# A two-block transformer kernel: first products by two tiles with the high parts first, router weights side by side, output-weight splits two steps later

## The reference

```
xn = layernorm(x)
x  = x + series_and_ffn(xn) + lora_top2(xn)          # block 0
xn = layernorm(x)
x  = x + attention(xn) + base_and_lora_routed(xn)    # block 1
```

## Time and profile before

| | us |
|---|---|
| median of 3 runs | 628.64 |
| lowest, highest | 627.43, 631.06 |
| the profiled execution | 631.41 |
| its span (first to last instruction) | 629.7 |
| mean granted clock of TensorE in it | 0.984 of full |

### The profile page before, as it was taken

How to read it: one execution, slowest core, us unless ns; L and a number is a source line. 1 busy time by engine, 2 the same in 40 slices (tenths; PEclk the granted TensorE clock), 3 DMA queues, 4 the chain that set the end, 5 groups by cost and what they waited for, 6 DMA issues and landing times.

```text
span 629.7 us, 9383 instructions
## 1 busy us (share of the span) xinstructions
PE 602.0 (96%) x3704; PEld 397.4 (63%) x3704; DVE 373.6 (59%) x553; ACT 293.3 (47%) x511; POOL 76.2 (12%) x106
## 2 busy tenths in 40 slices
PE   2999999999999999999999998999999999999996
PEld 2788888877888887687676764344444444534444
DVE  5667645237644324875845356568898888861225
ACT  3465524124523222423212114677787787756772
POOL 3000000000000000402211112121212122111210
PEclk9999999999999999999999998899999999969999
DMA  7424232312021212377914735161615440101003
GB/s 214 135 90 134 68 120 81 101 33 68 34 67 34 67 34 67 104 168 212 171 52 134 141 130 92 22 109 32 120 45 98 79 69 19 31 9 30 15 14 133
DMA packets 24067, 53.12 MB, mean 84 GB/s; under 512 B 8384, under 2 KB 8896, under 8 KB 24016
## 3 DMA queue, kind: packets, MB, share of 16 engines
q1 hardware_dynamic: 23736, 51.96, 32.3%
q0 software_dynamic: 288, 0.58, 0.4%
HBM read 39.63 MB, written 10.60 MB: 80 GB/s over the span
## 4 chain that ended last, share of the span: by engine, by line
PE 87%; ACT 5%; DVE 5%; issue 1%; DMA 1%; SPq 0%; DVEq 0%; ACTq 0%
PE bank L1289 12%; PE slot L1011 11%; PE slot L1013 10%; PE slot L1012 10%; PE bank L1272 10%; PE bank L1011 9%; PE bank L1013 8%; PE bank L1012 8%; PE slot L1183 6%; ACT probs L994 4%; PE slot L1191 2%; DMA x_sb<-in_x 1%; PE slot L1027 1%; PE slot L1272 1%; DVE maxcol L1637 1%
## 5 line engine op out<-in xcount | busy, mean ns | idle before, releaser
L994 ACT ACTIVATE probs<-bank 128x512 f32<-128x512 f32 (+2 forms) x294 | 144.2, 566 | 53.3 <-PE bank L1272 50.1
L1637 DVE TENSOR_REDUCE maxcol<-slot 128x2 f32<-128x1024 f32 (+2 forms) x112 | 125.1, 1142 | 31.2 <-PE slot L1183 16.2
L1011 PE MATMUL slot<-xt_hi,ring_hi 128*128 128x512 f32 (+2 forms) x248 | 98.3, 396 | 3.6 <-DVE xt_lo L1412 2.4
L1012 PE MATMUL slot<-xt_lo,ring_hi 128*128 128x512 f32 (+2 forms) x248 | 97.5, 393 | 0.0
L1013 PE MATMUL slot<-xt_hi,ring_lo 128*128 128x512 f32 (+2 forms) x248 | 97.4, 393 | 0.0
L1289 PE MATMUL bank<-probs,v_sb 128*32 128x512 f32 (+3 forms) x768 | 86.6, 525 | 0.1
L1272 PE MATMUL bank<-qst,kst 50*128 50x512 f32 (+3 forms) x275 | 74.5, 431 | 5.6 <-ACT probs L994 4.1
L1272 PEld LDWEIGHTS bank<-qst,kst 50*128 50x128 f32 x275 | 33.7, 193 | 63.7 <-ACT probs L994 51.5
L786 POOL TENSOR_SCALAR_AFFINE_SELECT probs<-probs 128x512 f32<-128x512 f32 x64 | 41.7, 652 | 188.0 <-ACT probs L994 187.9
L1637 DVE TENSOR_REDUCE maxrest<-slot 128x2 f32<-128x768 f32 (+3 forms) x48 | 49.8, 1045 | 21.9 <-PE slot L1191 21.7
L1183 PE MATMUL slot<-kst,qst 48*128 48x512 f32 (+3 forms) x288 | 57.0, 388 | 2.3 <-DVE negm L1650 2.0
(11 more groups left out here) (212 smaller groups left out, 851.2 us busy)
## 6 DMA issues: line engine op xcount, KB each, us to landing
stage<-in_stream SPq DMA_DIRECT2D x43, 512.0 KB, 3.5
qst<-heads_dram SPq DMA_DIRECT2D x12, 256.0 KB, 4.9
kst<-heads_dram SPq DMA_DIRECT2D x12, 256.0 KB, 7.9
heads_dram<-attn_hi SPq DMA_DIRECT2D x4, 512.0 KB
heads_dram<-attn_lo SPq DMA_DIRECT2D x4, 512.0 KB
out_y<-x_sb SPq DMA_DIRECT2D x8, 256.0 KB, 2.1
stage<-u_sb SPq DMA_DIRECT2D x56, 32.0 KB, 2.0
stage<-den_dram SPq DMA_DIRECT2D x14, 128.0 KB
```

The lines of the kernel that those rows point to most:

```text
L994: act.activation(probs[:, to:to + heads, 0:n], score_ps(b)[:, 0:heads * n].rearrange("p (h n) -> p h n", n=n), ACT.Exp, scale=HD ** -0.5). ...
L1011: pe.matmul(out_ap, a[0], b[0], start=start, stop=False)
L1012: pe.matmul(out_ap, a[0], b[1], start=False, stop=False)
L1637: dve.tensor_reduce(per_head[:, :, slots[0]:slots[-1] + 1], scores, AX.X, ALU.max).then_inc(S["max_free"], 1)
```

## The change

Four places. (1) Start: pairs 0 and 1 are turned into the four single banks instead of the slots; pair 0's copy on ACT and low part on DVE come ahead of pair 1's normalization; PE runs 20 transposes of the identity before turn(0) and 18 behind it; the first gate_up product is done for the 256 tokens of pair 0 first, high by high, then high weights by low tokens, then turn(1), then low weights by high tokens, then all of it for pair 1; weight item 2 is issued ahead of x tiles 4-7. (2) Half 1, chunk 0: two of the four take_outs move behind h_lo. (3) Router weights of block 1: high and low columns lie side by side (32 stationary columns), so high weights and low weights meet the high tokens in one matmul; the two parts are transposed and then added by a reduction; the eviction of the logits moves ahead of the value-weight splits. (4) Attention: wo0 is split at step 3 and wo1 at step 4 of group 0.

```diff
-SPLIT_AT = {(0, 1): "wo0", (0, 3): "wo1"}
+BEFORE_TURN, BEHIND_TURN = 20, 18
+SPLIT_AT = {(0, 3): "wo0", (0, 4): "wo1"}
 def psum_users():
-    users = [("x", 0), ("x", 1)]
+    users = []
...
-        lgt1 = probs[0:ROUTES_PAD, 0:2, :].rearrange("p a n -> p (a n)")
+        lgt1 = probs[0:2 * ROUTES_PAD, 0:2, :].rearrange("p a n -> p (a n)")
...
-            return slot_of(("x", q))[:, n, :] if q < 6 else bank[2 * (q - 6) + n][:, :]
+            return slot_of(("x", q))[:, n, :] if 2 <= q < 6 else bank[2 * (q % 2) + n][:, :]
...
             weights(1)
+            weights(2)
             sp.dma_start(x_sb[:, 4:8, :], x_in[4:8].rearrange("t p d -> p t d")).then_inc(S["x_landed3"], 16)
-            for n in range(2, item_at[("wv1", 0)] + 1):
+            for n in range(3, item_at[("wv1", 0)] + 1):
                 weights(n)
...
             std(0)
+            turned_hi(0)
             std(1)
-            turned_hi(0)
             split_hi(0)
             turned_hi(1)
+            split_hi(1)
             act.wait_ge(S["ratio_diff"], 1)
             act.activation(ratio[:], disc[:], ACT.Exp).then_inc(S["ratio_ready"], 1)
-            for n in range(1, 3):
-                split_hi(n)
+            split_hi(2)
...
+            def keep_clock(n):
+                for _ in range(n):
+                    pe.transpose(slot[1][:, 0, 0:P], ident[:], ident[:])
+
+            def first_gate_up():
+                n, hi, lo = ring_of("gate_up")
+                hi, lo = (t.rearrange("p (k m) -> p k m", k=KD) for t in (hi, lo))
+                ps = slot_of(("s", 0))
+                early = slice(0, 2 * P)
+
+                def part(w, x, start, stop):
+                    for out in range(2):
+                        for k in range(KD):
+                            pe.matmul(ps[:, out, early], w[:, k, out * P:(out + 1) * P], x[:, k, early],
+                                      start=start and k == 0, stop=stop and k == KD - 1)
+
+                pe.wait_ge(S["xt_hi_ready"], 1)
+                pe.wait_ge(S["w_hi"], 1)
+                part(hi, xt_hi, True, False)
+                pe.wait_ge(S["x_free"], 1)
+                part(hi, xt_lo, False, False)
+                turn(1)
+                pe.wait_ge(S["w_lo"], 1)
+                part(lo, xt_hi, False, True)
+                pe.wait_ge(S["x_free"], 2)
+                for out in range(2):
+                    last = from_xt(ps[:, out, 2 * P:HALF], (hi, lo), out * P, (out + 1) * P, 2 * P, 2 * P)
+                last.then_inc(S["s_ready"], 1)
+
             pe.wait_ge(S["ident_ready"], 2)
+            keep_clock(BEFORE_TURN)
             turn(0)
-            turn(1)
+            keep_clock(BEHIND_TURN)
...
             def route_logits(n):
-                return from_xt(slot_of(("r", 0))[0:ROUTES_PAD, n, :], (rw_hi, rw_lo), 0, ROUTES_PAD, n * HALF, HALF)
+                at = slice(n * HALF, (n + 1) * HALF)
+                for k in range(KD):
+                    pe.matmul(slot_of(("r", 0))[0:2 * ROUTES_PAD, n, :], rw[:, k].rearrange("p a n -> p (a n)"),
+                              xt_hi[:, k, at], start=(k == 0), stop=False)
+                    last = pe.matmul(slot_of(("r", 0))[0:ROUTES_PAD, n, :], rw[:, k, 0, :], xt_lo[:, k, at],
+                                     start=False, stop=(k == KD - 1))
+                return last
...
+                    src = logit[:, :, 0:routes]
+                    parts = wide(bank[0][:, 0:1], (2 * ROUTES_PAD, NT), (1, routes), (ROUTES_PAD, 2))
+                    then(dve.tensor_reduce(src, parts, AX.X, ALU.add))
...
             statistics(1)
+            turned_lo(0)
             invert_std(1)
             normalize(1)
-            turned_lo(0)
             split_lo(0)
             turned_lo(1)
+            split_lo(1)
             dve.wait_ge(S["vec_landed"], 64)
...
-            split_lo(1)
             split_lo(2)
...
                 if half == 1:
-                    for t in range(HT):
+                    for t in range(2):
                         take_out(t)
...
+                    if (half, c) == (1, 0):
+                        for t in range(2, HT):
+                            take_out(t)
                     if c == 0:
                         dve.wait_ge(S["l_a_ready"], half + 1)
                         route(HT, NE, half)
...
             for n in range(2):
                 first_lo(0, n)
+            dve.wait_ge(S["r_ready"], 1)
+            dve.tensor_scalar(lgt1, slot_of(("r", 0))[0:2 * ROUTES_PAD].rearrange("p a n -> p (a n)"),
+                              vec_sb[0:2 * ROUTES_PAD, VEC_ROUTER1:VEC_ROUTER1 + 1], None, ALU.add
+                              ).then_inc(S["r_free"], 1)
             for n in range(2):
                 split_lo(item_at[(f"wv{n}", 0)])
```

More of the change, by code:

```diff
@@ L816, in turned_hi @@
                 act.wait_ge(S["x_turned"], q + 1)
-                if q < 6:
+                if 2 <= q < 6:
                     act.activation(xt_hi[:, :, t:t + 2 * P].rearrange("p k (t n) -> p t k n", t=2),
@@ L1019, in turn @@
                 src = xn if q < 6 else xn_last[q]
-                if q < 6:
+                if 2 <= q < 6:
                     wait_slot(pe, ("x", q))
-                else:
+                elif q >= 6:
                     pe.wait_ge(S["out_free"], 2 * HT)
@@ L1043, in _ @@
             pe.wait_ge(S["ident_ready"], 2)
+            keep_clock(BEFORE_TURN)
             turn(0)
-            turn(1)
+            keep_clock(BEHIND_TURN)
             for half in range(2):
                 tok0 = half * HALF
[L1049 to L1054, removed]
+                if half == 0:
+                    first_gate_up()
+                else:
+                    pe.wait_ge(S["x_free"], 2 + 2 * half)
+                    w = weight("gate_up", half)
+                    ps = slot_of(("s", half))
+                    wait_slot(pe, ("s", half))
+                    from_xt(ps[:, 0, :], w, 0, P, tok0, HALF)
+                    from_xt(ps[:, 1, :], w, P, 2 * P, tok0, HALF).then_inc(S["s_ready"], 1)
@@ L1154, in _ @@
             for t in range(NT):
-                last = pe.transpose(bank[0][:, t * ROUTES_PAD:(t + 1) * ROUTES_PAD], lgt1[:, t * P:(t + 1) * P],
-                                    ident[0:ROUTES_PAD, 0:ROUTES_PAD])
+                last = pe.transpose(bank[0][:, 2 * t * ROUTES_PAD:2 * (t + 1) * ROUTES_PAD], lgt1[:, t * P:(t + 1) * P],
+                                    ident[0:2 * ROUTES_PAD, 0:2 * ROUTES_PAD])
             last.then_inc(S["lt_ready"], 1)
@@ L1416, in route @@
             def route(n_tok, routes, e):
-                src = slot_of(("l", e))[:, 1, 0:HT * NE] if e < 2 else bank[0][:, 0:NT * ROUTES_PAD]
-                w = NE if e < 2 else ROUTES_PAD
-                src = src.rearrange("p (t e) -> p t e", e=w)[:, :, 0:routes]
+                if e < 2:
+                    src = slot_of(("l", e))[:, 1, 0:HT * NE].rearrange("p (t e) -> p t e", e=NE)
+                else:
+                    src = logit[:, :, 0:routes]
+                    parts = wide(bank[0][:, 0:1], (2 * ROUTES_PAD, NT), (1, routes), (ROUTES_PAD, 2))
+                    then(dve.tensor_reduce(src, parts, AX.X, ALU.add))
                 then(dve.tensor_reduce(rowmax[:, 0:n_tok], src, AX.X, ALU.max))
@@ L1493, in take_out @@
                                   ).then_inc(S["out_free"], 1)
-            then(dve.tensor_copy(rw_hi[:].rearrange("p k n -> p (k n)"), rw_stage[:]))
-            dve.tensor_tensor(rw_lo[:].rearrange("p k n -> p (k n)"), rw_stage[:],
-                              rw_hi[:].rearrange("p k n -> p (k n)").bitcast(F32), ALU.subtract
-                              ).then_inc(S["rw_ready"], 1)
+            rw_f = rw_stage[:].rearrange("p (k n) -> p k n", k=KD)
+            then(dve.tensor_copy(rw[:, :, 0, :], rw_f))
+            dve.tensor_tensor(rw[:, :, 1, :], rw_f, rw[:, :, 0, :].bitcast(F32), ALU.subtract).then_inc(S["rw_ready"], 1)
             for half in range(2):
```

7 lines of the change are left out of this document (1 added, 6 removed).

## The result

The changed kernel takes **620.27 us** (median of 4 runs, 619.31 to 621.38), the kernel before, on the same chip, 629.85 (4 runs, 627.43 to 636.65). The ratio is 0.9863, 95% [0.9823, 0.9902]. The forecast of 622.1 is 1.8 too high, within its range, and "faster" is right: the interval leaves 1 out.

The account below looks back on a forecast made before the run. TensorE (PE), occupied for 96% of the span, was taken as the bound. Terms of -2.2, -0.45, -2.2 and -1.7 sum to -6.55 us, from the median 628.64 to 622.1; range 618.5 to 627.

Parts of the forecast that it names:

- Start: First products to second feed-forward chunk: warm clock and earlier products start that chunk at 29.7 instead of 31.94, -2.2 us.
- Rival (a): Start: warm-up transposes don't raise the clock; second chunk 1.9 us later than before, total 626.1; chance 0.27.
- Second half: Half 1's first chunk: moving two take_outs closes the 1.14 us hole, gate_x is late next, -0.45 us.
- Router: Router up to the first maxima: fewer products and an earlier eviction, -2.5 us for PE, -2.2 after a new wait.
- the loads: Last key loads before the first maxima: they come 0.85 us earlier, PE 2.5, so a new wait of 0.3 us.
- 1.63 for fewer products and 0.85 for the eviction: Router: 16 products for 24 save 0.7 and 0.93 us; the earlier eviction closes the 0.85 us hole before the transposes.
- Attention: First attention group: later output-weight splits gain 2.3 us at the hole, 0.6 given back to ACT, -1.7 us.
- the 2.3 booked for the hole: First attention group: negation follows the transpose at once, the 1.97 us hole goes, -2.3 us at this point.
- The 0.6 booked as lost to ACT: First attention group: the split behind step 4 takes ACT 1.06 us among dense exponentials; 0.6 us of it lost.
- Clock: Attention's low clock from 388.6 to 395.6: an earlier rise, worth at most 2.3 us, was not counted.
- rival (d): First attention group: the clock stays up where it fell at 388.6; 2.3 us below the forecast, 619.8; chance 0.09.
- rival (c): Attention: the clock falls more often, up to 0.5 us per low us; 14 us more eats 6.6; chance 0.06.

Follow-up runs that it names:

- No warm-up: Changed kernel with none of the 20 and 18 warm-up transposes: 622.88 us (6 runs), ratio 0.9878 to the kernel before.
- Take-outs alone: Kernel before with only half 0's output tiles 2 and 3 taken out behind h_lo of half 1's chunk 0: 631.09 us (one run).
- Combined: Changed kernel with output-weight splits as in "High part earlier", router split behind chunk 5, lora1 and q low parts before gate spreading: 623.11 us, ratio 0.9872.
- Hole filled: Kernel before with 16 identity transposes on PE in the first attention group, ahead of the maxima waiting for negm: 630.76 us (12 runs), ratio 1.0017.
- High part earlier: Changed kernel with ACT's output-weight splits back at steps 1 and 3, DVE's at 2 and 3: 619.95 us (6 runs), ratio 0.9813.
- the router alone: Kernel before with only the paired router weights, 32-row transposes and earlier logits' eviction: 633.7 us (12 runs), ratio 0.9982.
- the start alone: Kernel before with only the new start, warm-up and its order of ACT, DVE and SP included: 631.55 us (13 runs), ratio 0.999.
- the splits: Kernel before with only the output-weight splits moved behind steps 3 and 4 of attention group 0: 627.2 us (12 runs), ratio 0.9958.
- the twelve later executions: The changed kernel run again, nothing altered, to see how long the clock is low: 628.92 us (12 runs), ratio 0.9874.

## Why the forecast was right, and where it was not

**Start: -2.2 forecast, -2.2 measured** (leg A; 2.15 between the means of five traces and of six, 31.65 and 29.5). The warm start and PE's early arrival were right: PE waits 1.8 us for h_lo. But that 29.75 met 29.7 is luck: delta came 0.9 us earlier than booked and the chain behind it took 0.8 longer, since the weights do not keep up as the prediction said. What ends last there is a weight item's DMA, through ACT's copy; where it comes sooner leg A goes down to 29.0. Rival (a) is refuted by rows: turn(0) at 1.11 us behind the 20 transposes, 1.94 without them. The Trainium skill says in "TensorE: Matmul & The Clock Gate", Part 4 (PE-mode transpose), that the high clock doesn't engage for transposes; this trace shows it engage during them, and the measurement decides. The rival's price of 4.1 us against the forecast was not tested in full, as "No warm-up" has no 18 transposes at the low level ahead of the first product. Without them the second chunk came 1.1 us later: the spacing fell to 0.12 us at about 13.8, where the rival had it low to the end.

**Second half: -0.45 forecast, -0.7 to -0.8 measured** (leg B). gate_x took the hole's place as forecast, with a wait of 0.37 us. "Take-outs alone" shows it without any other part.

**Router: -2.2 forecast, -1.6 measured.** PE's gain up to the transposes was well sized (2.5 against 2.6). The step that failed is what is late next: I took it to be the loads and booked 0.3 for them. Counted from the transposes of gate_x the last are issued 0.2 us earlier and not 0.85, but the larger ones land in 6.4 us (median) where they took 8.8, so by about 283.2, 3 us ahead of the first maxima. PE waits instead for attn_lo, 15 us behind the transposes: DVE has the spreading of the gates (1.66 us) and a weight split (1.22) ahead of it, and PE now arrives 2.6 us earlier. "Combined" takes this wait away and has 2.6 in full. The other lesson is how the parts hang together: I summed 1.63 for fewer products and 0.85 for the eviction, while with the eviction in its old place the fewer products gave 0.2. The earlier eviction with the old weights was not run.

**Attention: -1.7 forecast, -2.8 measured to the first value product** (leg F). Of the 2.8 about 0.4 is clock: between the end of the hole and the first value product PE needs 0.97 us at the low level, and 0.56 for the same instructions at the high one in "Hole filled". The rest, 2.4, is the 2.3 booked for the hole. The 0.6 booked as lost to ACT lies behind leg F. PE waits for exponentials 2.0 us in the steps up to the scores near 399, where the same steps had 1.5 before, and ACT's split at its old place takes 0.3 of it away ("High part earlier"). So 0.3 of the 0.6 is shown; G lies on the same line for both kinds of kernel, within the 0.5 us of that line.

**Clock: 0 forecast, -4.1 in this pair** (leg G; 10.4 us less at the low level there, by the line 3.7). In direction that is rival (d), but not by its mechanism: the clock still falls in the first group, just for 3.4 us, and the 10.2 us at 556 are absent. The size belongs to the execution: the changed kernel has 3.7 to 48 us of it in 16 runs, the kernel before 10 to 50 in 52. Whether the change also shifts the odds, as rival (c) feared, is open: 30 us or more at the low level had 10 of 52 runs before, 6 of 16 of the changed kernel, 7 of 12 with the router alone and 5 of 13 with the start alone. The price in (c), up to 0.5 for each us, was 0.36.

So the sum of the change's own steps is -7.3 in the legs (-2.2 - 0.8 - 1.6 + 0.05 - 2.8) against a forecast of -6.55, and the remaining -4.1 of the pair's 11.4 is the clock. The runs give a second estimate: each time less 0.357 us for each us at the low level comes to 617.5 in the mean for the changed kernel (16 runs), 622.7 for the one before (52), 622.0 for the start alone, 621.2 for the splits, 621.1 for the router, 619.1 without warm-up, 616.0 for "combined" and 624.4 with the hole filled. The errors of these means are 0.1 to 0.4 us. By this the change is worth 5.2 us, 1.3 less than the forecast, and the start alone 0.7 and not the 2.0 of its leg A; why so little is not known. Part of the gap to 7.3 is known: the low clock before lies partly on the hole, where it costs nothing, and the line charges it (2 us, 0.7). The rest is 1.4, and the profiled execution before, with 631.41, is itself 1.2 above the mean of the ten others of the same granted clock, 0.984 (630.2, spread 0.8). So that pair may overstate the change by about that. The median of 9.6 less in the first comparison holds 2 to 4 us that other executions give back. So the total was met by luck too: of the twelve later executions only three were at the low level for so short a time as the first four. "Combined" is the best version at equal clock, by 1.5 us against the changed kernel; its ratio to the kernel before does not separate it from that.

What brings the clock down at about 383 to 396 us in most executions, and for how long, could not be settled.

## What to carry to other kernels

Cut a trace into legs between instructions that all variants have: legs that repeat to 0.15 us let one trace settle what ten timed runs leave open, and show which leg holds the noise. Where an edit shortens one engine's queue, read what the next instructions wait for on every other engine, not on the DMA queues alone, and expect the edit to be worth nothing until that engine's order follows. Read the granted clock of the leg too before you call its length the edit's. When a forecast moment is met, check the moments ahead of it: two errors can cancel. Before you book a difference of totals, read the granted clock of each execution: here it moved the time by three times what the change did.

## What the runs showed of the hardware

Transposes alone raised TensorE to its high level: 20 of an identity, back to back from 1.58 us (3.86 us for 20, then 1.11 us for eight in place of 1.94). After an idle stretch of 2.39 us behind eight transposes the next products ran at the low level (2.04 us for eight, in one execution), while 18 transposes in the same place kept them at the high one (1.19).

In the attention the granted clock fell to 0.5 for 3.4 to 44 us at a time, the first time at 383 to 396 us in eleven of the thirteen traces, also where PE had had no wait but one of 0.73 us in the 7 us before, and in different lengths in executions of one and the same kernel. Each us there cost 0.36 us, less than the half that PE's rate would make it; that other engines set part of the pace would explain it, and isn't shown.
